# The second group's low-rank projections: transposed raw tiles and float32 passes on TensorE in place of VectorE's dot products, with the first group's order changed around them

## What is computed

```
def _qlora_linear(x, wq, A, B):
    w = jnp.tile(wq, (1, 4))
    base = x @ w.T
    lora = x @ A.T @ B.T
    return base + lora * LORA_SCALING
...
gate = jax.nn.silu(_qlora_linear(x, w1q, a1, b1))
up = _qlora_linear(x, w3q, a3, b3)
return _qlora_linear(gate * up, w2q, a2, b2)
...
xn = _layernorm(x, axis=-1)
s = _L0_attn_ref(xn)
g = _silu(_L0_ffn_ref(xn, ...))
x = x + s * g
```

## Time and profile before

| what | value |
|---|---|
| device time, median of 3 runs | 875.64 us (874.33 to 876.18) |
| profiled execution: its own time | 875.03 us |
| its span in the profile | 873.0 us |
| PE busy | 836.9 us (96%) |
| DVE busy | 627.7 us (72%) |
| ACT busy | 307.4 us (35%) |
| POOL busy | 301.1 us (34%) |
| mean granted TensorE clock | 0.985 |

### The profile page before, as it was taken

One profiled execution on the slowest core, in us unless ns is written; L12 is line 12 of the kernel. 1 busy time (PEld: TensorE's weight loads), 2 busy tenths in 40 slices (PEclk: granted clock), 3 DMA queues, 4 the chain that ended last, 5 costly groups with the idle time before them and its releaser, 6 DMA issues.

```text
span 873.0 us, 11158 instructions
## 1 busy us (share of the span) xinstructions
PE 836.9 (96%) x4078; PEld 435.7 (50%) x4078; DVE 627.7 (72%) x983; ACT 307.4 (35%) x456; POOL 301.1 (34%) x399
## 2 busy tenths in 40 slices
PE   5769969999999999999999999999999999999997
PEld 4323347443673347534584446743475345744366
DVE  6759895679758887679866797578876788644534
ACT  5746434433323332233323333223322333222221
POOL 5761661434404442145504344044431465000000
PEclk9989988999999999999999999999999999999999
DMA  9842004311232113500143113321135111320003
GB/s 287 280 153 56 10 29 142 128 36 31 56 139 80 37 30 75 190 24 26 48 129 121 37 32 55 132 86 37 31 71 190 22 31 17 112 100 1 1 1 145
DMA packets 51543, 70.03 MB, mean 80 GB/s; under 512 B 34976, under 2 KB 36864, under 8 KB 51216
## 3 DMA queue, kind: packets, MB, share of 16 engines
q1 hardware_dynamic: 51472, 69.18, 25.8%
HBM read 44.52 MB, written 16.78 MB: 70 GB/s over the span
## 4 chain that ended last, share of the span: by engine, by line
PE 88%; DVE 6%; issue 1%; DVEq 1%; POOL 1%; DMA 1%; ACT 1%; SPq 0%; POOLq 0%
PE g L1203 25%; PE u L1203 23%; PE zb L1295 6%; PE g L1354 5%; PE u L1354 5%; PE u L1363 4%; PE u L1361 4%; PE g L1363 4%; PE g L1361 4%; PE g L1221 3%; DMA xf<-in_x 1%; PE mb L1259 1%; DVEq L846 1%; PE u L1357 1%; PE g L1357 1%
## 5 line engine op out<-in xcount | busy, mean ns | idle before, releaser
L559 ACT ACTIVATE sil<-g,winv 128x512 f32<-128x512 f32 (+1 forms) x176 | 120.0, 683 | 284.5 <-PE g L1221 245.4
L1203 PE MATMUL g<-xt,w_h 128*128 128x512 f16 x672 | 202.1, 382 | 3.1 <-DVE xt L1085 2.7
L1203 PE MATMUL u<-xt,w_h 128*128 128x512 f16 x672 | 200.2, 380 | 2.2 <-DVE w_l L1049 2.2
L830 DVE SCALAR_TENSOR_TENSOR h<-u,winv,sil 128x512 f32<-128x512 f32 x168 | 125.5, 748 | 97.2 <-ACT sil L559 83.8
L785 DVE CUSTOM_DVE_ANT_0 junk<-xn,abc 128x1024 bf16<-128x1024 f32 x112 | 154.8, 1382 | 7.5 <-issue 2.2
L458 POOL TENSOR_TENSOR ve<-mv,three 128x1 f32<-128x1 f32 x32 | 6.5, 203 | 362.0 <-DVE mv L767 362.0
L1203 PE MATMUL g<-xt,w_l 128*128 128x512 f16 x336 | 127.9, 381 | 0.0
L1203 PE MATMUL u<-xt,w_l 128*128 128x512 f16 x336 | 127.3, 379 | 0.0
L1203 PEld LDWEIGHTS u<-xt,w_h 128*128 128x128 f16 x672 | 65.8, 98 | 82.9 <-DVE w_l L1049 2.7
L1203 PEld LDWEIGHTS g<-xt,w_h 128*128 128x128 f16 x672 | 57.3, 98 | 90.2 <-issue 34.0
L967 DVE SCALAR_TENSOR_TENSOR ob<-xr,c_mean,gg 128x1024 f32<-128x1024 f32 x27 | 34.7, 1284 | 62.1 <-ACT gg L559 41.5
(11 more groups left out here) (226 smaller groups left out, 1233.1 us busy)
## 6 DMA issues: line engine op xcount, KB each, us to landing
xr<-in_x SPq DMA_DIRECT2D x32, 512.0 KB, 4.5
out_x<-ob SPq DMA_DIRECT2D x31, 512.0 KB, 2.9
xf<-in_x SPq DMA_DIRECT2D x30, 512.0 KB, 3.5
raw_w<-in_w2t SPq DMA_DIRECT2D x1, 2560.0 KB
abc<-in_a SPq DMA_DIRECT2D x1, 2048.0 KB, 15.5
raw_w<-in_w1t SPq DMA_DIRECT2D x2, 768.0 KB, 7.9
raw_w<-in_w3t SPq DMA_DIRECT2D x2, 768.0 KB, 9.2
raw_w<-in_w1t SPq DMA_DIRECT2D x1, 704.0 KB, 11.5
```

Of the source, the lines that this page charges most:

```text
L559: return nc.scalar.activation(out, in_, f, **kw)
L830: stt(out=h[0:n, p % NH, :], in0=up, scalar=winv[0:n, 3 * block_of(p) + 1:3 * block_of(p) + 2], in1=sil[0:n, p % 2, :], op0=ALU.mult, op1= ...
L1203: o = mm(bank[:], a, x, start=opens and t == 0, stop=closes and t == len(terms) - 1)
```

## The change

z of group 1 is no longer made by dot products. TensorE transposes the raw tiles of group 1 in eight halves (`second_x(q, half)`, four 128x128 float32 transposes each, into `mb`, after pairs 3, 4, 6, 7, 12, 14, 17 and 19 of group 0 by the table `X_AT`); ScalarE copies each half out of `mb` to `xT1`, which lies where `abc` will lie. In the down stage of group 0, `second_z0` spreads 1/deviation and runs 16 float32 products, and `second_spread` spreads the scaled result; VectorE and ScalarE then split it into `zst`. `abc` is loaded only after that. Since `mb` has new users, the tables of the small work in group 0 move, and each user waits for the one before. The three copies to `a2st` move forward in GpSimd's queue; `w2_low(0)` and `w2_low(1)` move from the down stage to pairs 16 and 18; the first gate chain takes its six waits one at a time; `rsb`, `w_bound(1, 1)` and `w_high(1, 0)` move back in ScalarE's prologue. Groups 2 to 7 are unchanged.

```
-        aT = sb("aT", [P, 8, 32], F32, at=hf_at + 16384)
+        aT = sb("aT", [P, 8, 32], F32, at=zs_at)
...
+        xT1 = sb("xT1", [P, 8, G], F32, at=abc_at)
...
-        STATS_AT = [(3, 11, 17, 19)] + [(1, 7, 13, 19)] * (NG - 1)
-        NORM_AT = [(4, 12, 18)] + [(2, 8, 14, 20)] * (NG - 1)
-        Z_AT = [{p: (n // 4, n % 4) for n, p in enumerate((5, 8, 9, 10, 13, 14, 15, 16, 18, 19, 20, 21))}]
...
-        C_AT = [(9, 12)] + [(5, 9)] * (NG - 1)
-        I_AT = [(14, 17)] + [(11, 15)] * (NG - 1)
+        STATS_AT = [(3, 6, 11, 16)] + [(1, 7, 13, 19)] * (NG - 1)
+        NORM_AT = [(8, 13, 17)] + [(2, 8, 14, 20)] * (NG - 1)
+        Z_AT = [{}] + [{3 + 6 * q + r: (q, r) for q in range(3) for r in range(4)}] * (NG - 1)
+        X_AT = {3: (0, 0), 4: (0, 1), 6: (1, 0), 7: (1, 1), 12: (2, 0), 14: (2, 1), 17: (3, 0), 19: (3, 1)}
+        W2L_AT = {16: 0, 18: 1}
+        C_AT = [(11, 13)] + [(5, 9)] * (NG - 1)
+        I_AT = [(15, 18)] + [(11, 15)] * (NG - 1)
...
-        HIGH_AT = {1: ((1, 1),), 5: ((2, 0),), 6: ((2, 1),), 8: ((3, 0),), 9: ((3, 1),)}
+        HIGH_AT = {1: ((1, 0), (1, 1)), 5: ((2, 0),), 6: ((2, 1),), 8: ((3, 0),), 9: ((3, 1),)}
...
-        W2_AT = {13: 0, 14: 1, 15: 2, 16: 3, 17: 4, 19: 5}
+        W2_AT = {13: 0, 15: 1, 16: 2, 18: 3, 19: 4, 20: 5}
...
-            sp.dma_start(abc[:].rearrange("p r c -> p (r c)"),
-                         d["a13"].rearrange("r c -> (r c)").partition_broadcast(P)).then_inc(abc_loaded, 16)
...
+                if i == 0:
+                    sp.wait_ge(z0_ready, 3)
+                    sp.dma_start(abc[:].rearrange("p r c -> p (r c)"),
+                                 d["a13"].rearrange("r c -> (r c)").partition_broadcast(P)).then_inc(abc_loaded, 16)
...
+            raw_differences(FIRST_DIFF[0])
+            pool.wait_ge(c_loaded, 16 * 3)
+            for u in range(3):
+                cp(a2st[:, :, 2 * u:2 * u + 2], raw_a2[:]).then_inc(a2_done, 1)
+            for q in FIRST_DIFF[1:3]:
                 raw_differences(q)
...
             raw_differences(FIRST_DIFF[3])
-            pool.wait_ge(c_loaded, 16 * 3)
-            for u in range(3):
-                cp(a2st[:, :, 2 * u:2 * u + 2], raw_a2[:]).then_inc(a2_done, 1)
...
+            def second_x(n):
+                q, half = n // 2, n % 2
+                act.wait_ge(x1_ready, n + 1)
+                A(xT1[:, 4 * half:4 * half + 4, q * P:(q + 1) * P],
+                  mb[:].rearrange("p (k t) -> p k t", k=4), ACT.Copy).then_inc(x1_done, 1)
...
             quarter_normal(3)
-            act.wait_ge(rsb_ready, 1)
-            A(rsb[:], mb[:], ACT.Copy).then_inc(rsb_done, 1)
             w_high(0, 0)
...
             w_high(0, 1)
+            act.wait_ge(rsb_ready, 1)
+            A(rsb[:], mb[:], ACT.Copy).then_inc(rsb_done, 1)
...
             b_cast(0, 1)
-            w_bound(1, 1)
             act.wait_ge(z0_rest, 1)
             A(z_part[1][:], z_rest[:], ACT.Copy).then_inc(z0_part, 1)
+            w_bound(1, 1)
             b_scale(0)
-            w_high(1, 0)
...
                         if p in W2_AT:
                             w2_high(W2_AT[p])
+                        if p in X_AT:
+                            second_x(2 * X_AT[p][0] + X_AT[p][1])
...
+            def second_z():
+                dve.wait_ge(rsb_done, 2)
+                dve.wait_ge(z0_ready, 3)
+                tt(zc1[:], gb[0][:], rsb[:], ALU.mult).then_inc(zc_done, 1)
+                dve.wait_ge(z0_part, 3)
...
             w_low(0, 0, 0)
-            w_low(0, 0, 1)
             xt_low(0)
             xt_low(1)
+            w_low(0, 0, 1)
...
+                        if p in W2L_AT:
+                            w2_low(W2L_AT[p])
...
-                    dve.wait_ge(zeroed, 11)
-                    w2_low(0)
+                    flag(0)
+                    w2_low(2)
                 tail_sums(i)
...
                 z2_stack(i)
-                if not last:
-                    last_projections(i + 1)
...
+                if i == 0:
+                    second_z()
+                else:
                     if not last:
+                        last_projections(i + 1)
...
+            def first_gate():
+                for k in range(2):
+                    pe.wait_ge(wh_done, 1)
+                    pe.wait_ge(xth_done, k + 1)
+                    mm(gb[0][:], wt_h[0][:, k, 0:P], xt[:, k, :], start=k == 0, stop=False)
+                    pe.wait_ge(xtl_done, k + 1)
+                    mm(gb[0][:], wt_h[0][:, k, 0:P], xt[:, 2 + k, :], start=False, stop=False)
+                    pe.wait_ge(wl_done, k + 1)
+                    mm(gb[0][:], wt_l[0][:, k, 0:P], xt[:, k, :], start=False, stop=False)
...
+            def second_x(q, half):
+                n = 2 * q + half
+                buf, loaded, count = front_buf(1, q)
+                pe.wait_ge(loaded, count)
+                if n == 0:
+                    pe.wait_ge(z0_rest, 1)
+                else:
+                    pe.wait_ge(x1_done, n)
+                if n == 2:
+                    pe.wait_ge(wall_read, 3)
+                elif n in (4, 5):
+                    pe.wait_ge(sq_done, n - 3)
+                elif n in (6, 7):
+                    pe.wait_ge(gap_done, n - 5)
+                for k in range(4):
+                    c = P * (4 * half + k)
+                    o = nc.tensor.transpose(mb[:, k * P:(k + 1) * P], buf[:, c:c + P], ident[:])
+                o.then_inc(x1_ready, 1)
+
+            def second_z0():
+                pe.wait_ge(dev_done, 24)
+                pe.wait_ge(flag_read, 1)
+                for q in range(4):
+                    o = nc.tensor.transpose(mb[:, q * P:(q + 1) * P], rs[:, q:q + 1].broadcast_to([P, P]), ident[:])
+                o.then_inc(rsb_ready, 1)
+                pe.wait_ge(x1_done, 8)
+                pe.wait_ge(mult_done, at_pair(0, LAST))
+                for half in range(2):
+                    t = slice(256 * half, 256 * half + 256)
+                    for k in range(8):
+                        s = 32 * (k % 4)
+                        o = mm(gb[0][s:s + 32, t], aT[:, k, :], xT1[:, k, t], start=k < 4, stop=k >= 4)
+                o.then_inc(z0_ready, 1)
+
+            def second_spread():
+                pe.wait_ge(zc_done, 2)
+                mm(ub[0][:], sel[:], zc1[:], start=True, stop=True).then_inc(z0_ready, 1)
...
                     if i == 0 and p == 5:
+                        pe.wait_ge(x1_done, 2)
                         scale_sum(2, mb, 0)
...
+                    if i == 0 and p in X_AT:
+                        second_x(*X_AT[p])
...
                     down_high(0, range(3, HN))
+                    second_z0()
                     down_high(1, range(0, HN))
+                    second_spread()
                     down_low(0)
                     down_low(1)
+                    pe.wait_ge(zst_done, 2)
...
-                if not last:
+                if i and not last:
                     z_across(i + 1)
```

91 lines of the change are left out of this document (62 added, 29 removed).

## The result

The changed kernel takes 877.05 us (median of 7 runs, 876.77 to 878.02), the kernel before 875.14 us in the same comparison (873.29 to 876.18). The ratio is 1.0028, with a 95% interval of 1.0017 to 1.004: 0.28% slower, where I had predicted 869.3 us with a range that ended at 874.5. The profiled execution took 876.85 us, with a span of 874.7.

What follows compares the result with a forecast made beforehand. TensorE is busy throughout from 160 to 840 us, so only delays in group 0 up to the first pass of down(0, 2) count. 875.03 - 5.3 (that pass earlier) - 0.35 (z_across(1)) = 869.3 us, range 863.0 to 874.5.

Steps and rivals of the forecast that it cites:

- ScalarE runs gates 0 and 1 ahead of `w_high(1, 0)`, so products 0 and 1 end near 32.2 and not 36.3: Start of group 0: reordered ScalarE work lets VectorE's first two products end near 32.2 us instead of 36.3.
- nothing visible: Rival, chance 0.10: a2st copies wait for DMA, or ScalarE's backlog takes back 4 of 8.6 us; 873.3 to 877.4 us.
- slower: Rival, chance 0.07: GpSimd's tile 3 work lengthens VectorE's tail 6 to 9 us, TensorE stands throughout; 876 to 880.
- First `z2`, 45.5: Group 0: z2(0, 0) starts at 45.5 us, not 54.15, 8.6 earlier, with no wait for a2st.
- Waits in `mb`: Group 0's bank: 0.3 us each after pair 7 and before pair 11, 2.4 after pair 17, 3.7 after 19.
- The clock, 4.8 in two spells: Group 0: the 3.7 us wait and one near 2.4 each bring a 1.2 GHz spell; 4.8 us, range 0 to 7.2.
- From the first `z2` to the end of product 21: Group 0: from 45.5 to 106.2 us before clock spells; pair 21 ends at 104.4, its product 1.8 behind.
- From the end of product 21 to the mark, 21.7: Group 0's tail: from 106.2 us to the first pass of down(0, 2) at 127.9, before any slow spell.
- The stand of 2.3 us at the spread: Group 0's down stage: TensorE stands at second_spread from 118.1 to 120.4 us for VectorE's zc; 4.35 becomes 2.3.
- The mark, 132.7: First pass of down(0, 2) in group 0: at 132.7 us with clock spells, 5.3 earlier than before.
- `abc` and the reload: Around the first store: loading abc there, with tile 2's reload behind it, costs nothing; 2.8 us of cover before.
- The rule on SBUF: Argument against the edit: GpSimd blocks the moved w2_low operations, lengthening both gap waits; the sum kept 1.21 us each.

Runs made afterwards that it cites:

- experiment 1: Changed kernel with VectorE's wait for the tenth count of zeroed moved from ahead of group 0's products to the down stage: 870.85 us, ratio 0.9943.
- experiment 5: Kernel of experiment 1 with w2_low(0), w2_low(1) and the fourth stats behind VectorE's gap readings: 865.67 us, ratio 0.9896.
- experiment 6: Kernel of experiment 1 with the spread of the second group's z behind the ten passes of down_low(0): 869.74 us, ratio 0.9925.
- experiment 4: Kernel of experiment 1 with the a2st copies back behind the third raw difference: 877.34 us, ratio 1.0015.
- experiment 11: Changed kernel, its zeroed wait left as it was, with 43 idle instructions in VectorE's never-taken branch of group 0: 877.12 us, ratio 1.0013.
- experiment 3: Kernel before with only the three a2st copies moved forward, behind GpSimd's first raw difference: 868.78 us, ratio 0.992.
- experiment 7: Kernel of experiment 5 with the last half tile behind pair 20 and the flag's sum behind pair 21: 862.63 us, ratio 0.9845.
- experiment 9: Kernel of experiment 7 with 43 idle instructions in VectorE's never-taken branch of group 0: 859.15 us, ratio 0.9813.

## Why the prediction was wrong, point by point

**The step that failed** is the sentence "ScalarE runs gates 0 and 1 ahead of `w_high(1, 0)`, so products 0 and 1 end near 32.2 and not 36.3". It follows ScalarE and TensorE, which were both ready, and leaves out VectorE's third wait, for `zeroed`. Product 0 started at 40.65; in experiment 1, which moves only this wait, products 0 and 1 ran from 30.25 to 31.66. I had looked at where the memset of `zs` went and asked who needs `zs`; I did not ask what the counts behind it now mean. Among the rivals there was none with this wait. Two of them have 877 us in their span ("nothing visible" up to 877.4, "slower" from 876 to 880), but what they rest on is not in the trace: `a2st` was filled by 30.82, TensorE's waits for ScalarE's copies came to 0.65 us, and it did not stand at the spread.

**The rest, read where the wait is put right (experiment 1).** The prediction counts three spells at 1.2 GHz in the kernel before in one place and four in another; the windows show four. The pass count behind its 2.4 us for a spell is 12 and not eleven, which makes 2.3.
- *First `z2`, 45.5*: 45.66. The waits forecast at 0.6 and 0.9 for ScalarE's copies were 0.66 and 0.65 in the profile of experiment 5, and not to be seen in that of experiment 1. It had instead what the forecast had not, a spell of low clock (40 to 44 us at 0.60, some 1.6 us) behind the wait of 2.21 us for the low weights of block 1. Experiments 5 and 6, with the same code up to there and no such spell, had the first `z2` at 42.79 and 43.56. So the agreement is partly luck, and the forecast was some 2 us late for an execution in which the clock holds.
- *Waits in `mb`*: 2.4 forecast after pair 17 and 3.7 after pair 19; 1.98 and 4.58 in experiment 1, 1.97 and 5.45 in the changed kernel. The second was 5.4 to 5.5 in four of the five profiles that keep this order (the changed kernel and experiments 4, 6 and 11); experiment 1 is the one below. Those after pair 7 and before pair 11 were not there. A wait of 1.12 at pair 9, for product 8, was, and I had none for it. In sum 7.7 for 6.7.
- *The clock, 4.8 in two spells*: the windows of experiment 1 have 0.96 from 60 to 100 us and 0.94 from 100 to 160, so 1.6 + 3.6 = 5.2. Spells came behind both waits. The 1.6 named above come on top of these. In the changed kernel the same windows have 1.00 and 0.97, so 1.8: there the wait of 1.97 was not followed by a spell.
- *From the first `z2` to the end of product 21*: 45.5 to 106.2, and 4.8 for the clock, makes 65.5. Experiment 1 has 66.43 (45.66 to 111.34 + 0.75).
- *From the end of product 21 to the mark, 21.7*: 20.84 in the changed kernel (118.35 to 139.19) and in experiment 1 (112.09 to 132.93). The sum is near and its parts are not. The stand of 2.3 us at the spread was absent: TensorE's own work up to it is 13.3 us, not 11.9, and VectorE's tail 13.3, not 14.1. The terms that the prediction names for TensorE (2.4, 2.5 and 4.6) reach 115.7, not its 118.1. In experiment 1 the last `z2` and the chunks took 6.2 where it named 2.4 (112.09 to 118.24), `second_z0` 2.4 and the twenty passes 4.8. This stretch is 0.9 shorter than forecast and the one before it 0.9 longer, so they cancel in the mark.
- *The mark, 132.7*: 132.93.
- *The time, 869.3*: 870.85, of which two waits of TensorE behind the stand in the fifth group, which I had not seen coming, are 1.8 + 0.6 in the profiled run.
- *`abc` and the reload*: no wait of TensorE at the start of group 1, as forecast.

**The rule on SBUF** (the Trainium skill, SBUF — State Buffer, Who interferes with whom) did bear on the gap, and the 1.21 that the sum went by was too little in the changed kernel. `w2_low(1)` took 2.14 us there. It began within a two-input operation of GpSimd, which also took 1.70 in place of the 1.28 that the same operation has in experiment 1:

```profile
104.28 2.14 DVE L1113 TENSOR_TENSOR w_l<-raw_w,w_h 128x1024 fp32r<-128x1024 f32 x1
```

```profile
103.64 1.70 POOL L522 TENSOR_TENSOR yh<-xn 128x512 f32<-128x512 f32 x1
105.42 1.59 POOL L524 TENSOR_TENSOR xq<-yh 128x256 f32<-128x256 f32 x1
```

In experiment 1 it took 1.26, and the wait behind it was 4.58 and not 5.45: 0.87 us of wait for 0.88 us of operation. There it started first, and GpSimd's next two-input operation, which took 0.67 in the changed kernel, took 1.52:

```profile
98.34 1.26 DVE L1113 TENSOR_TENSOR w_l<-raw_w,w_h 128x1024 fp32r<-128x1024 f32 x1
```

```profile
98.60 1.52 POOL L530 TENSOR_TENSOR hl<-xq,hl 128x256 f16<-128x256 f32 x1
```

By the rule the one that comes second is blocked until the first is done. Experiment 1 agrees. In the changed kernel GpSimd's operation came first and VectorE's was the longer for it, as the rule has it, but GpSimd's was longer too (1.70 for 1.28), which the rule doesn't give. `w2_low(0)` took 1.22 in the changed kernel and in experiment 1, so nothing of this met it.

**What the change is worth.** The copies of `a2st` alone bring 0.8% (experiment 3). The rest of the change brings nothing beside them, until VectorE's and TensorE's order around the gaps is changed too (experiments 5 and 7). With both and the code moved (experiment 9, 859.15 us) it is 1.9% below the kernel before, and faster than any kernel here without the transposed tiles. How much of that is z on TensorE stays open: no run has it without the new order of the prologue, and none tries a better order around VectorE's waits on the kernel of experiment 3.

## What to carry to other kernels

A wait on a counter names a number, not an event. When an edit takes out or moves an operation that increments it, read every wait on that counter again and write down which operation each number now stands for; a number that the edit leaves as it was can now stand for another operation. And when one late wait is taken away, look for a second one that reaches the same place: at 54 us TensorE waited for `a2st`, and could be held by the products as well, so taking away one and adding the other came out almost even.

Try the cheapest edit of a change by itself. Here three copies made the gain, and what was added beside them had to be paid for in waits before it paid.
